# Counting labels on VectorE instead of TensorE in a gated graph network kernel

## What is computed

```python
labels = jnp.arange(1, D + 1, dtype=adj.dtype)
mask = (adj[None] == labels[:, None, None, None]).astype(dt)
weight = mask / (jnp.sum(mask, axis=-1, keepdims=True) + EPS)
agg = jnp.einsum('dbmn,bnh->bmdh', weight, hid).reshape(hid.shape[0], hid.shape[1], D * H)
out = jax.nn.relu(_linear(agg, Wd, bd))
r = jax.nn.sigmoid(_linear(out, Wri, bri) + _linear(hid, Wrh, brh))
z = jax.nn.sigmoid(_linear(out, Wzi, bzi) + _linear(hid, Wzh, bzh))
n = jnp.tanh(_linear(out, Wni, bni) + r * _linear(hid, Wnh, bnh))
out = (1.0 - z) * n + z * hid
mu, var = jnp.mean(out, axis=-1, keepdims=True), jnp.var(out, axis=-1, keepdims=True)
return (out - mu) / jnp.sqrt(var + LN_EPS) * gamma + beta
```

## Time and profile before

| | |
|---|---|
| median of 3 runs | 511.12 us (510.72 to 511.8) |
| the profiled execution | 511.09 us, span 509.3 us |
| TensorE busy | 492.2 us, 97% |
| VectorE busy | 431.3 us, 85% |
| ScalarE busy | 421.4 us, 83% |
| GpSimd busy | 370.0 us, 73% |
| DMA | 33.42 MB, mean 66 GB/s |

### The profile page before, as it was taken

One profiled execution on the slowest core, in us unless ns is written; L12 is line 12 of the kernel. 1 busy time (PEld: TensorE's weight loads), 2 busy tenths in 40 slices (PEclk: granted clock), 3 DMA queues, 4 the chain that ended last, 5 costly groups with the idle time before them and its releaser, 6 DMA issues.

```text
span 509.3 us, 10652 instructions
## 1 busy us (share of the span) xinstructions
PE 492.2 (97%) x2951; PEld 447.3 (88%) x2951; DVE 431.3 (85%) x1077; ACT 421.4 (83%) x819; POOL 370.0 (73%) x369
## 2 busy tenths in 40 slices
PE   8999699999999999999999999999999999999992
PEld 4789588999999999999999999999999999999892
DVE  5899979888888888888888888889888888988877
ACT  5878678888888898888888888888988888897772
POOL 2889677777787777778777777877777787775535
PEclk9999799999999999999999999999999999999997
DMA  8310222111222211122221111222111222110111
GB/s 275 128 53 1 82 84 74 54 51 48 68 74 72 72 52 51 44 70 72 72 72 51 51 49 64 72 72 72 53 50 43 71 72 72 51 41 23 42 42 62
DMA packets 20261, 33.42 MB, mean 66 GB/s; under 512 B 2256, under 2 KB 6992, under 8 KB 20240
## 3 DMA queue, kind: packets, MB, share of 16 engines
q1 hardware_dynamic: 19872, 32.38, 19.3%
q10 hardware_dynamic: 288, 0.52, 0.3%
q0 software_dynamic: 80, 0.26, 0.1%
HBM read 24.77 MB, written 8.39 MB: 65 GB/s over the span
## 4 chain that ended last, share of the span: by engine, by line
PE 88%; DVE 8%; issue 1%; DMA 1%; ACT 1%; POOL 0%; SPq 0%; POOLq 0%; ACTq 0%; DVEq 0%
PE y_bank L412 26%; PE alpha L412 24%; PE gamma L412 13%; PE p_bank L449 12%; PE beta L412 10%; PE t_bank L457 3%; DVE masks L1179 1%; DMA adj_in<-in_adjT 1%; PE t_bank L438 1%; DVE wx_lo L1194 1%; DVE y_lo L1204 1%; DVE y_lo L1280 1%; DVE shared L1189 0%; DVE wd_lo L1210 0%; DVE ratio L1220 0%
## 5 line engine op out<-in xcount | busy, mean ns | idle before, releaser
L449 PE MATMUL p_bank<-y_hi,masks 128*128 128x256 f32 x256 | 67.2, 284 | 0.8 <-DVE y_lo L1204 0.4
L449 PE MATMUL p_bank<-y_lo,masks 128*128 128x256 f32 x256 | 66.8, 283 | 0.0
L1847 POOL TENSOR_TENSOR x_lo<-x_f,x_hi 128x1024 fp32r<-128x1024 f32 x27 | 65.0, 2407 | 1.6 <-ACT x_hi L1014 1.6
L1850 POOL TENSOR_TENSOR y_lo<-shared,y_hi 128x512 fp32r<-128x512 f32 x28 | 36.5, 1303 | 25.2 <-ACT y_hi L1037 25.2
L1836 POOL TENSOR_TENSOR var_eps<-mean_var,ln_eps 128x2 f32<-128x2 f32 x27 | 5.2, 194 | 65.4 <-DVE mean_var L1454 65.4
L449 PEld LDWEIGHTS p_bank<-y_hi,masks 128*128 128x128 f32 x256 | 48.4, 189 | 4.0 <-DVE y_lo L1204 1.3
L449 PEld LDWEIGHTS p_bank<-y_lo,masks 128*128 128x128 f32 x256 | 48.5, 190 | 1.3
L412 PE MATMUL y_bank<-wd_hi,x_hi 128*128 128x512 f32 x112 | 47.1, 421 | 0.2
L985 ACT ACTIVATE p_bank<-p_bank,ratio 128x256 f32<-128x256 f32 x112 | 45.2, 448 | 0.0
L412 PE MATMUL y_bank<-wd_lo,x_hi 128*128 128x512 f32 x112 | 44.5, 397 | 0.0
L412 PE MATMUL y_bank<-wd_hi,x_lo 128*128 128x512 f32 x112 | 44.3, 396 | 0.0
(11 more groups left out here) (315 smaller groups left out, 1798.2 us busy)
## 6 DMA issues: line engine op xcount, KB each, us to landing
x_f<-in_xT SPq DMA_DIRECT2D x32, 256.0 KB, 2.6
x_rows<-in_x SPq DMA_DIRECT2D x32, 256.0 KB, 2.6
out<-shared SPq DMA_DIRECT2D x31, 256.0 KB, 2.0
adj_in<-in_adjT SPq DMA_DIRECT2D x32, 128.0 KB, 2.0
shared<-in_wgT SPq DMA_DIRECT2D x2, 576.0 KB, 6.4
shared<-in_wdT ACTq DMA_DIRECT2D x2, 256.0 KB, 5.0
vec_rows<-in_vectors SPq DMA_DIRECT2D x1, 512.0 KB, 7.0
shared<-in_wgT SPq DMA_DIRECT2D x2, 192.0 KB, 7.1
```

The costliest lines, as they stand in the source:

```text
L449: last = nc.tensor.matmul(p_bank[:, b * H:(b + 1) * H], masks[:, k % 2, g, d, :], part[:, g, d * H:(d + 1) * H], start=first, stop=(part i ...
L1847: nc.gpsimd.tensor_tensor(*split_lo(x_lo[:, k % XRING, :, :], x_f[:, k % 2, :, :], x_hi[:, k % XRING, :, :])).then_inc(xlo_ready, 1)
L1850: nc.gpsimd.tensor_tensor(*split_lo(y_lo[:, EVEN, half(1)], u3_y[:, :], y_hi[:, EVEN, half(1)]))\
```

## The change

The host makes a second copy of the adjacency, not transposed (`adjN`, the node itself on the partitions). From pair 5 on (`CS`), its rows for the pair are loaded into the place of `zeros_bf`, by one more transfer a step on the sync queue, behind the store. VectorE compares them with each label and lets the same instruction sum the result along the row (`accum_out`): eight instructions a step of 128 x 128, the comparison's result going to a part of `t_bank` that nobody reads, the sum to the column of `t_bank` where TensorE's product put it. Four stand in front of mask 2, four in front of mask 3. `counted` is no longer called for these pairs, and TensorE's wait for the masks moves to the first label product that uses them.

```diff
+        adj_rows = zeros_bf[:, :].bitcast(i32).rearrange("p (g n) -> p g n", g=2)
...
                     sp.dma_start(out[up(j)].rearrange("p (g f) -> p g f", g=2), normed[:, j % 2, :, :])\
                         .then_inc(stored[j % 2], 16)
+                k = i + 1
+                if k >= CS and has_pair(k):
+                    if k > CS:
+
+                        sp.wait_ge(found_ready, up(2 * D * (k - CS), 2 * D))
+                    sp.dma_start(adj_rows, adjN[up(k)].rearrange("p (g m) -> p g m", g=2)).then_inc(adj_rows_loaded, 16)
...
                     product(q, alpha, A11, B11).then_inc(p1_done, 1)
-                    pe.wait_ge(masks_ready, up(D * (i + 1), D))
-                    counted(i)
                 pe.wait_ge(u3y_ready, up(n))
...
                 pe.wait_ge(yl22_ready, up(n))
+                if n >= 2:
+                    pe.wait_ge(masks_ready, up(D * (i + 1), D))
                 p_products(i, 0, False)
...
+                def count(g):
+
+                    for d in range(D):
+                        c = g * D + d
+                        if c >= 3:
+
+                            dve.wait_ge(found_ready, up(2 * D * (i - CS) + c - 2, 2 * D))
+                        place = (1 + c % 3) * N
+                        nc.vector.tensor_scalar(t_bank[:, place:place + N], adj_rows[:, g, :], float(d + 1), None, ALU.is_equal, ALU.add,
+                                                accum_out=t_bank[:, g * D + d:g * D + d + 1]).then_inc(found_ready, 1)
+
...
                     nc.vector.tensor_tensor(mix[:, :], z_part[:, :], n_sb[:, :], ALU.add).then_inc(mix_ready, 1)
+                    dve.wait_ge(adj_rows_loaded, up(16 * (i - CS + 1), 16))
+                    dve.wait_ge(ohi_ready, up(i - 1))
+                    dve.wait_ge(relu_ready, up(i - 1))
+                    count(0)
                     mask(i, 2)
...
+                    count(1)
                     mask(i, 3)
...
-                dve.wait_ge(count_done, up(i + 1))
+                if n == 1:
+                    dve.wait_ge(count_done, up(i + 1))
+                else:
+                    dve.wait_ge(found_ready, up(2 * D * (i - CS + 1), 2 * D))
...
+    adjN = np.asarray(adj).reshape(PAIRS, 2, N, N).transpose(0, 2, 1, 3).reshape(PAIRS, N, 2 * N)
```

More of the change, by code:

```diff
@@ L18 @@
 YPAIRS = PAIRS - YS
+CS = YS + 1
 FIRST = 6
@@ L36, with gnn_kernel @@
 SUMS = ASKED[4:]
-def gnn_kernel(nc, x, xT, adjT, wdT, wgT, bd, vectors, out):
+def gnn_kernel(nc, x, xT, adjT, adjN, wdT, wgT, bd, vectors, out):
     f32, f32r, bf16, i32 = mybir.dt.float32, mybir.dt.float32r, mybir.dt.bfloat16, mybir.dt.int32
@@ L149, in gnn_kernel @@
         adj_loaded = [sem("adj_loaded0"), sem("adj_loaded1")]
+        adj_rows_loaded = sem("adj_rows_loaded")
         rows_loaded = [sem("rows_loaded0"), sem("rows_loaded1")]
@@ L184, in gnn_kernel @@
         counts_ready = sem("counts_ready")
+        found_ready = sem("found_ready")
         rcount_ready = sem("rcount_ready")
@@ L1953 @@
         "x": np.ascontiguousarray(rows), "xT": np.ascontiguousarray(xT), "adjT": np.ascontiguousarray(adjT),
+        "adjN": np.ascontiguousarray(adjN),
         "wdT": np.ascontiguousarray(wdT), "wgT": np.ascontiguousarray(wgT),
```

## The result

The changed kernel takes 537.5 us (median of 4 runs, 536.65 to 537.78) against 511.36 us before: 1.0508 times as long, 95% interval 1.0496 to 1.052, or 26.1 us more. Forecast were 546.2 us within 517 to 566.

What follows compares the result with a forecast made beforehand. TensorE's instruction stream was taken to set the step, 14.86 us. Less 0.30, plus 2.16 of counting beyond 0.56 free on VectorE, gives 16.16; 27 x 1.30 = 35.1 us added to 511.1 gives 546.2 us, range 517 to 566.

Steps and rivals of the forecast that it cites:

- The bound moves from TensorE to VectorE, and the stall stands at line 1483: TensorE's weight load before a y product waits for VectorE's line 1483 once a step, about 1.6 us.
- TensorE gives up 0.30 us a step: Removing the eight counting products shortens TensorE's step by 0.30 us, 8.1 us over 27 steps if nothing else becomes late.
- The price of a count, 0.27: On VectorE, start to start: 0.20 us for the stream plus 0.07 for the sum, between 0.135 and 0.39.
- D: VectorE's added counting time a step, eight counts: 2.16 us, between 1.08 and 3.12; the step becomes 14.00 + D.
- The masks cost what they did: VectorE's masks, 0.20 us each, kept their time unsaid; GpSimd's shift by half of D was costed at nothing.
- The gap in front of the second `labels_first`, 0.36: VectorE's wait for TensorE before the second line 1425 absorbs 0.36 us; with 0.20 slack at the load, 0.56 is free.
- After the stall TensorE runs as before: Behind the once-a-step stall TensorE was to keep its old timing up to the next start of line 1425.
- P: Start of VectorE's line 1425 (256.11) after TensorE's last label product of the first graph; VectorE's way to 1483 begins there.
- A free sum: Rival on a count's price: the sum costs nothing, 0.20 to 0.22 us each, 531 to 535 us; chance 0.28.
- the dear sum: Rival: the sum's read-out waits for the stream, 0.39 us a count, 572 us; taken from 0.33, 557 us upwards; chance 0.15.
- the masks' rate: Rival: the stream runs as fast as the masks, sum free, 0.135 us a count, 517 us, up to 525; chance 0.08.
- the other side: Rival: counts fit almost entirely between existing operations at 0.07 us each, TensorE never waits, 503 us; chance 0.05.

Runs made afterwards that it cites:

- e4: Changed kernel with only the four counts of the first graph of each pair made (second graph's counts wrong for pairs 5 to 31): 514.47 us, ratio 1.0062.
- e1: Changed kernel with the counting products gone, nothing counting in their place for pairs 5 to 31, and no second copy loaded: 503.06 us, ratio 0.9843.
- e2: Changed kernel with the eight comparisons kept but without the sum (counts wrong for pairs 5 to 31): 533.29 us, ratio 1.0436.
- e3: Changed kernel with the first four counts moved in front of masks 0 and 1, nothing left out: 528.79 us, ratio 1.034.
- e5: Changed kernel with GpSimd's last split of the step done for 256 of its 512 columns: 528.78 us, ratio 1.0343.
- e6: Changed kernel with comparison results written to SBUF as bytes and sums to a small SBUF tile, nothing left out: 537.32 us, ratio 1.0512.
- e7: As e6, but counting the next pair in VectorE's idle places, five counts before the relu sums, three before c22; second copy loaded before the store: 520.36 us.
- e8: As e7, with six waits fewer a step on VectorE (masks 1 to 3 no longer repeat mask 0's two waits): 519.33 us, ratio 1.0167.
- e10: As e8, with the hardware loop written out on every engine, 24 steps in a row: 504.5 us, ratio 0.9865 to the kernel before.

## Why the prediction was right

**The bound moves from TensorE to VectorE, and the stall stands at line 1483.** Shown: 27 waits of TensorE, all for the y sum (now line 1510), 1.2 us each where 1.6 were forecast; the wait in front of the second `labels_first` is gone, that in front of the relu sums a little under half of what it was. e4 adds that the loss follows the number of counts.

**TensorE gives up 0.30 us a step.** Shown by e1: 8.2 us measured, 8.1 forecast.

**The price of a count, 0.27.** It was mis-sized, though inside its bounds. It is 0.207: 0.193 for the stream, against 0.20, and 0.014 for the sum, against 0.07 (e2). The Trainium skill (VectorE: DVE Perf Modes, section "Two Vector instructions with no wait between them") has the sum as an instruction of its own, and the trace agrees: 216 reads of the accumulator. What the forecast made of an instruction more, 0.07, is what failed; the read hides behind the comparison. D is 1.66 instead of 2.16, 0.50 less.

**The masks cost what they did.** This was assumed without a word, with GpSimd's shift costed at nothing, and is wrong. With the new rhythm they meet GpSimd's last split and take 0.76 instead of 0.40; 0.36 more a step in that row, 0.32 by the times of e3 and e5, since the overlap is shorter at the loop's returns. The prediction asked of GpSimd only what it is late for, never what it runs beside. The margin of 0.06 us before stood in the trace. The Trainium skill (Advanced Engine Details and Errata, section "GPSIMD Details") says that GpSimd shares a read and a write interface with VectorE and conflicts with its instructions in a two-port mode. The traces agree as far as they go: e3 and e5 show a conflict in which VectorE's masks wait, and the counts show none, since in e3 they start beside the split that ends at 265.69 and still go at 0.205 each. In which mode either runs is shown by no run.

**The gap in front of the second `labels_first`, 0.36.** Two more rows of the kernel before are needed here and in the next paragraph:

```profile
260.19 0.68 DVE L1468 TENSOR_TENSOR shared<-gamma,shared 128x512 f32<-128x512 f32 x1
...
270.97 0.48 DVE L1425 SCALAR_TENSOR_TENSOR out_rows<-p_bank,rcount,bd_rows 128x256 f32<-128x256 f32 x1 [0.15 <-PE p_bank L449]
```

The gap is 0.44 from start to start: line 1468 starts at 260.19, an operation of 512 columns lets the next one start after 0.60 (line 1445), and line 1425 starts at 261.23. So 0.08 more is absorbed.

**After the stall TensorE runs as before.** Before, it was 6.73 us from the weight load (264.24) to the next P (270.97), and 0.05 for the step from one engine to the other: 6.78. Measured from the end of line 1510 (260.74) to the next P (267.38): 6.64, 0.14 less. Of this 0.12 lies at the product that was waited for, which starts with its load: the one behind it starts 0.34 after that load, where before it was 0.46 (264.24 to 264.70).

Together: 16.16 - 0.50 + 0.36 - 0.08 - 0.14 = 15.80 us, the step that the timeline shows (260.06 to 275.86). Two errors of opposite sign, 13.5 us and 9.7 us over 27 steps, cancelled in large part, and that is luck; a forecast with the right price and no contention would have been 511.1 + 27 x (1.66 - 0.86) = 533 us, 4.8 too low. The mechanism, the place of the stall and the range do not rest on that luck.

**What is hidden.** ScalarE's line 1027 was named as the next to be late. It is. It is hidden, since the copy behind it (line 1035, now 1046) ends at 261.21 and TensorE's first product behind the three passes starts at 261.59, with no wait for it in the list:

```profile
259.58 0.60 ACT L1038 ACTIVATE mix<-shared 128x512 f32<-128x512 f32 x1 [1.37 <-DVE shared L1502]
```

The second copy costs nothing: in the list of waits nobody waits for it, and its transfers land in 2.2 us.

```profile
zeros_bf<-in_adjN SPq DMA_DIRECT2D x27, 128.0 KB, 2.2
```

**The rivals.** A free sum was given 531 to 535 us and is almost what happened to the price, at 0.207 within its 0.20 to 0.22; the time fell outside by the contention. Of the others, the dear sum is excluded by e2, the masks' rate by e2 and e6, the other side by e4. One border in the prediction is a slip: 0.33 a count gives 511.1 + 27 x (2.64 - 0.86) = 559 us and not 557; no conclusion changes.

## What to carry to other kernels

Work taken from a full engine is only gained if the engine that takes it has room at the place where the first one waits for it: here VectorE had 1.8 us of idle time a step, but on its way to the y sum only 0.64 of the 1.66 us of counting found room, until the counts were moved (537 us against 504.5, the latter with the loop written out). Price an instruction in a busy engine from start to start, and when it delays an engine, ask also which operation of another engine it will now run beside. If a moved version stalls at the return of a loop, look at the row of the instruction queue too, and run the loop written out once, with a control.

## What was not expected of the hardware

- The read of an accumulator on VectorE is 0.08 to 0.09 us long, yet the sum with its read adds only 0.014 us from start to start. A comparison with a sum takes 0.207 us for 128 columns, as 32-bit numbers into PSUM and as bytes into SBUF alike, where a mask without a sum, SBUF to SBUF, takes 0.20 for 256.
- Two masks that start beside a GpSimd operation on 128x512 take 0.76 us instead of 0.40: what is left of that operation, and 0.27 us more.
- In e7 and e8 VectorE stands still for up to 2.8 us at each return of the hardware loop, and the instruction queue moves 38 packets instead of 13; the changed kernel, with more instructions than e8, has neither. Why it does so in these two is open; that instructions are fetched anew is suggested by the packets and not shown. That the return is what brings it on is shown by e10.
